# Routing weights of the first experts by broadcast transfers instead of a matrix product, with a third bank and longer rings

## Chip, cores and metric

The program runs on one core of a Trainium2 chip. The metric is the device time of one execution in microseconds (us), the median over the runs shown. The engines are named as in the profile: PE (matrix products; PEld is its weight load), DVE (vector), ACT (activation functions), POOL (the general engine), SP (which here only issues transfers).

## What is computed

A stack of eight blocks works on 2 x 1024 tokens of width 128, each block adding its normed result to the running stream. The change touches the sixth, a layer of experts:

```python
topk_w = topk_w / (topk_w.sum(-1, keepdims=True) + 1e-20)
combine_w = (jax.nn.one_hot(topk_idx, E, dtype=x.dtype) * topk_w[..., None]).sum(1)
g = jnp.einsum('th,eih->tei', x, gate_proj)
u = jnp.einsum('th,eih->tei', x, up_proj)
act = jax.nn.silu(g) * u
y = jnp.einsum('tei,ehi,te->th', act, down_proj, combine_w)
sg = x @ shared_gate_w.T
su = x @ shared_up_w.T
y = y + jax.nn.silu(sg) * su @ shared_down_w.T
```

There are E = 16 experts with 176 hidden rows each, and two shared experts (352 rows). Each token uses four of the sixteen, with the weights `combine_w`; the other twelve have weight zero. The kernel computes all sixteen for all tokens and multiplies by the weight, which is zero for most.

## The kernel before, in words

**Tiling.** The 16 x 176 + 352 hidden rows, padded, are 25 tiles of 128 rows (`R2`). The tokens are four chunks of 512 (`NC`, `CH`); chunks 0 and 1 are batch 0, chunks 2 and 3 are batch 1. The stage is one loop of 100 steps, i = 25 c + r: chunk c, tile r in the order `ORDER5`. The first three tiles of each chunk (`SHARED5 = 3`) are shared experts and need no routing weight; the other 22 are "weighted" steps. A tile of 128 rows holds rows of one expert or of two, since 176 is no multiple of 128: of the 22 tiles, 14 hold rows of two.

**A step.** fp32 values are split in a rounded part and a rest, so each product is three matmuls of 128 x 128 by 128 x 512. In step i, PE does the gate product (`pe_parts`, lines 1719 to 1721) into bank i % 2, the up product (the same lines) into bank 2 + i % 2, in a weighted step the spread (line 1768: a 0/1 matrix `SEL2` times the turned weights `CWT`, which copies each expert's weight of each token to all its rows, into bank 4), and then the down product of step i - 2 (`pe_hidden_parts`, lines 1725, 1726, 1728), which adds up over a chunk in bank 5. ACT takes the SiLU of the gate (line 1827, semaphore `sg`) and rounds the hidden value (line 1815, `hi`). DVE multiplies the SiLU by the weight (line 1874, `t`, reads bank 4), subtracts the rounded part of the step before (line 1863, the rest, `h`), and multiplies by the up product (line 1881, `p`), in that order. The times below speak of p(i), the start of line 1881 in step i. `um` says that the up product, and in a weighted step the spread, is done; `gm` says it of the gate; `dm` of the down product.

**What waits for what.** The rounded hidden value and its rest are rings of two (`HD5`, `HL5`), the SiLU a ring of two (`SG5`), the hidden value a ring of two (`PR5`). PE's gate of step i waits for `sg` of step i - 2, its up for `p` of step i - 2, the spread for `t` of the weighted step before, the down product of step i - 2 for `hi` and, ahead of its last matmul, for `h`. After the last tile of a chunk ACT copies bank 5 out (line 1819, `ot`, at r = 2 of the next chunk), and the down product of tile 0 of the next chunk waits for it.

**Other work in the loop.** `pe_beside_moe5`, `act_beside_moe5` and `dve_beside_moe5` insert, at fixed steps, the routing of batch 1 (DVE, chunk 0, r = 4, 8, 12, 16), the turning of the weights (PE and ACT, r = 1 for batch 0, r = 20 and 21 for batch 1), the norm of the finished chunk (DVE r = 5 and 6, then POOL, then PE's `pe_turn_x` at r = 9), and the attention features of the next block (PE r = 11 and 15, ACT r = 12 and 16, DVE r = 13 and 16; ACT changes its function table there and back). In chunk 2 PE also does `pe_lin_kv`, `pe_lin_out` and `pe_lin_proj` (r = 18, 20, 23).

**The weights.** `dve_route5_d` ends with the weights of a batch, in three bf16 parts (`dve_bf16_parts`, lines 1547 to 1550). PE turns them (line 1584), and ACT copies them to `CWT` (line 1590, `cwTs`).

**Transfers.** SP issues, in program order, the loads of this stage's matrices long before it, then during chunk 3 the loads of the eighth block's matrices (`moe3a`, `moe3b`, `r3w`), each behind a wait on PE's progress (`sp_late`). POOL splits them (lines 1686 and 1688) as they land.

Of the kernel before, what the change touches and what calls it, by code (L numbers as in the profile page):

```python
# [65 lines left out]
def sandwich(nc, x, w, cols, rows, rope, fc1q, fc2q, s2row, l1int, l2fc, r2w, r2b, moe2, moe2sel,  # L66
             r3w, r3b, moe3a, moe3b, consts, out):
    ctx = ExitStack()
    with ctx:
# [1079 lines left out]
        def sp_late(sp):  # L1149

            sp.wait_ge(A[1, "pv"], QH * KT * NG)
            for part, loads in enumerate((
                    ((LI, l1int),),
                    ((L2A, l2fc[:, 0:512]), (L2B, l2fc[:, 512:1024]), (arena(3328, 48), r2w), (arena(3376, H + D), r2b)),
                    ((MG, moe2[0]), (MU, moe2[1]), (MD, moe2[2]), (SEL2, moe2sel.bitcast(BF16))))):
# [1444 lines left out]
```

## Time and profile before

| | |
|---|---|
| median of 3 runs | 1651.7 us (1648.27 to 1655.72) |
| profiled execution, device time | 1657.76 us |
| its span in the trace | 1656.0 us |
| granted PE clock, mean of the span | 0.88 |
| the stage of the change, in the trace | 1111.3 to 1395.8 us |
| busy over the whole span: PE, DVE, ACT, POOL | 79%, 65%, 69%, 16% |

A busy share is the sum of the durations of an engine's instructions. PE's matmuls overlap, so that the distance between two starts says what one costs, not its duration. In a row of the timeline the bracket at the end gives the idle time before the instruction and what ended it.

### The profile page before, as it was taken

What the parts mean: (1) busy time and instruction counts of PE and PEld (TensorE: products, weight loads), DVE (VectorE), ACT (ScalarE), POOL (GpSimd) and SP (SyncE); (2) the same over time, 40 slices, a digit from 0 to 9 for tenths busy, and PEclk for the clock granted to TensorE, in tenths of its full rate; (3) what the DMA queues carried; (4) which work ended last, traced back from release to release, by engine and by line L of the source; (5) the groups of instructions that cost most, each with busy time, mean ns of one, the idle gap of its engine ahead of it and who ended that gap; (6) DMA issues with size and microseconds to landing.
All of it is one profiled execution on the core that took longest, in us unless ns stands there. A gap on an engine that the chain in (4) does not pass through costs nothing.

```text
span 1656.0 us, 22190 instructions
## 1 busy us (share of the span) xinstructions
PE 1315.9 (79%) x8121; PEld 659.1 (40%) x8156; DVE 1083.6 (65%) x2048; ACT 1147.4 (69%) x1619; POOL 261.9 (16%) x361
## 2 busy tenths in 40 slices
PE   5599988885777777777777696779998888787996
PEld 3233333353111111111111244466666666565774
DVE  6977777154446645664665645469876777676887
ACT  3166767655999999999999644444565455867884
POOL 4400003031000000000000123461101024611000
PEclk9589999997687887788788898879999989999998
DMA  5511110004210100010000210000000002000000
GB/s 191 136 22 21 29 34 4 1 1 111 80 20 0 20 19 1 20 20 0 20 1 0 111 58 0 1 1 1 1 1 1 1 13 96 1 1 1 7 8 13
DMA packets 22748, 44.07 MB, mean 27 GB/s; under 512 B 3248, under 2 KB 7600, under 8 KB 21872
## 3 DMA queue, kind: packets, MB, share of 16 engines
q1 hardware_dynamic: 21776, 41.09, 8.9%
q10 hardware_dynamic: 864, 1.57, 0.3%
q8 instruction: 64, 1.05, 0.3%
q14 instruction: 44, 0.36, 0.1%
HBM read 28.89 MB, written 13.76 MB: 26 GB/s over the span
## 4 chain that ended last, share of the span: by engine, by line
PE 43%; ACT 24%; DVE 19%; issue 11%; POOL 3%; ACTq 0%; DMA 0%; POOLq 0%; another core or an unknown queue 0%; DVEq 0%
ACT SHARED L1033 14%; PE PS L821 4%; PE PS L990 4%; PE PS L977 3%; DVE SHARED L1043 3%; DVE NM L730 3%; PE PS L1719 3%; PE PS L1721 3%; PE PS L1720 3%; PE PS L710 2%; PE PS L643 2%; PE PS L1725 2%; PE PS L785 2%; PE PS L1728 2%; PE PS L1726 2%
## 5 line engine op out<-in xcount | busy, mean ns | idle before, releaser
L1033 ACT ACTIVATE SHARED<-PS 128x1536 f32<-128x1536 f32 (+1 forms) x352 | 466.1, 1434 | 31.2 <-PE PS L977 30.2
L977 PE MATMUL PS<-QS,KS 51*128 51x512 bf16 (+1 forms) x1024 | 242.1, 461 | 134.1 <-ACT SHARED L1033 128.7
L1043 DVE TENSOR_TENSOR SHARED<-SHARED 128x1536 f32<-128x1536 f32 (+1 forms) x176 | 286.6, 1703 | 86.4 <-ACT SHARED L1033 86.4
L801 ACT ACTIVATE SHARED<-PS 128x512 f32<-128x512 f32 (+3 forms) x384 | 164.5, 493 | 99.3 <-PE PS L789 89.0
L977 PEld LDWEIGHTS PS<-QS,KS 51*128 51x128 bf16 (+1 forms) x1024 | 41.1, 99 | 386.8 <-ACT SHARED L1033 358.7
L990 PE MATMUL PS<-SHARED,Vg 128*16 128x512 f32 x1024 | 157.9, 694 | 1.7 <-DVE SHARED L1043 1.6
L730 DVE TENSOR_REDUCE NM<-PS 128x2 f32<-128x1024 f32 (+3 forms) x128 | 129.0, 1022 | 27.7 <-PE PS L716 19.6
L1719 PE MATMUL PS<-ROUNDED 128*128 128x512 f32 x328 | 141.6, 432 | 6.7 <-DVE SHARED L2194 3.5
L1721 PE MATMUL PS<-ROUNDED 128*128 128x512 f32 x328 | 132.3, 403 | 0.0
L1720 PE MATMUL PS<-ROUNDED 128*128 128x512 f32 x328 | 131.6, 401 | 0.0
L1827 ACT ACTIVATE KS<-PS 128x512 f32<-128x512 f32 x100 | 59.9, 599 | 84.8 <-PE PS L1721 84.3
L1725 PE MATMUL PS<-ROUNDED 128*128 128x512 f32 x228 | 109.0, 478 | 9.9 <-ACT SHARED L1819 6.1
L474 POOL COPY Vg<-XH 128x256 f32<-128x256 f32 x16 | 6.4, 402 | 628.6 <-PE PS L990 396.9
L324 POOL TENSOR_SCALAR VEY<-MVY 128x4 f32<-128x4 f32 x32 | 7.6, 237 | 619.8 <-DVE MVY L265 618.6
L821 PE MATMUL PS<-SHARED,Vg 128*16 128x256 f32 (+3 forms) x1152 | 96.0, 407 | 11.1 <-ACT SHARED L801 9.6
L2205 DVE TENSOR_TENSOR ROUNDED<-KS,ROUNDED 128x512 fp32r<-128x512 f32 x103 | 74.9, 731 | 42.4 <-ACT ROUNDED L2136 41.3
L2130 ACT ACTIVATE KS<-PS,C 128x512 f32<-128x512 f32 x103 | 71.1, 691 | 37.6 <-PE PS L1721 37.1
L1728 PE MATMUL PS<-ROUNDED 128*128 128x512 f32 x228 | 92.7, 407 | 4.3 <-DVE ROUNDED L2205 3.8
L710 PE MATMUL PS<-SHARED 48*128 48x512 bf16 (+3 forms) x384 | 72.0, 374 | 29.2 <-DVE NM L730 18.3
L1815 ACT ACTIVATE ROUNDED<-KS 128x512 fp32r<-128x512 f32 x100 | 62.9, 629 | 44.9 <-DVE KS L1881 44.2
L1874 DVE TENSOR_TENSOR SHARED<-KS,PS 128x512 f32<-128x512 f32 x88 | 60.1, 683 | 49.1 <-ACT KS L1827 45.8
L1726 PE MATMUL PS<-ROUNDED 128*128 128x512 f32 x228 | 91.3, 401 | 0.0
(280 smaller groups left out, 2352.2 us busy)
## 6 DMA issues: line engine op xcount, KB each, us to landing
qx<-SHARED SPq DMA_DIRECT2D x24, 256.0 KB, 4.0
SHARED<-in_moe SPq DMA_DIRECT2D x3, 1600.0 KB, 12.8
kx<-SHARED SPq DMA_DIRECT2D x18, 256.0 KB, 3.9
SHARED<-qx SPq DMA_DIRECT2D x16, 192.0 KB, 4.6
SHARED<-kx SPq DMA_DIRECT2D x16, 192.0 KB, 5.2
QS<-qx SPq DMA_DIRECT2D x16, 192.0 KB, 4.5
KS<-kx SPq DMA_DIRECT2D x16, 192.0 KB, 4.9
kx<-SHARED ACTq DMA_DIRECT2D x6, 256.0 KB, 5.2
```

The lines of the kernel that those rows point to most:

```text
L730: dve.tensor_reduce(out=dst, in_=src, axis=AX.X, op=ALU.max, negate=True).then_inc(A[0, "a_red"], 1)
L801: act.activation(PB[t % 3][:, h, q0:CH], bank(RING0[n % 3], q0), ACT.Exp, scale=SCORE_SCALE)\
L821: ins = pe.matmul(PS[32 * h:32 * h + VC, 6 * CH + a:6 * CH + b], Vg[g % 2][:, kt, h, :], PB[t % 3][:, h, a:b], start=kt == 0, stop=last an ...
L977: ins = pe.matmul(bank((v % 2) * GRP + f - a), KS[g % 2][r, h // 2, kt * P:kt * P + P], QS[g % 2][r, h // 2, qh * CH:(qh + 1) * CH], start ...
L990: ins = pe.matmul(PS[32 * h:32 * h + VC, 6 * CH:7 * CH], Vg[g % 2][:, kt, h, :], EX[:, f * CH:f * CH + CH], start=kt == 0, stop=kt == KT - 1)
L1033: act.activation(dst, PS[:, (v % 2) * GRP * CH:((v % 2) * GRP + b - a) * CH], ACT.Exp if second == qh else ACT.Sigmoid, scale=SCORE_SCALE)\
L1043: dve.tensor_tensor(ex_tile(j), ex_tile(j), GR[w % RING][:, 0:(b - a) * CH], ALU.mult)\
L1719: pe.matmul(dst, w[0], x[0], start=start, stop=False)
L1720: pe.matmul(dst, w[0], x[1], start=False, stop=False)
L1721: return pe.matmul(dst, w[1], x[0], start=False, stop=stop)
L1725: pe.matmul(dst, w[0], x[0], start=start, stop=False)
L1728: return pe.matmul(dst, w[0], x[1], start=False, stop=stop)
```

## The change

The spread on PE and its 0/1 matrix go away, and with them the three bf16 parts: the weights stay fp32 (`CW5`), are turned as fp32 by PE, copied by ACT into `WT5` (16 x 1024), and written by SP to DRAM (`wx`, 16 x 2048), once for each batch. For each of the 88 weighted steps SP then loads a 128 x 512 tile in which the row of an expert is repeated over the partitions of its rows: one transfer for each owner of the tile, so 36 a chunk and 144 in all. Four slots (`WB5`) form a ring: slot n is loaded when `p` of weighted step n - 4 is done. DVE multiplies the SiLU by the slot in place. Bank 4, now free, becomes a third bank of up products; `HD5`, `HL5` become rings of three, and the down products run three steps behind (`LAG5`). SP's loads of the eighth block stand between the weight loads of chunk 3, and `r3w` comes last.

```diff
+        wx = nc.dram_tensor("wx", (E2, TOK), F32, kind="Internal").ap()
-        SEL2 = ARENA[:, 13184:14784].bitcast(BF16)
+        WB5 = [arena(13184 + CH * i, CH) for i in range(3)] + [arena(32256, CH)]
...
+            def sp_experts7(r):
+                for name, part, dst, src in early.get(r, ()):
+                    sp.wait_ge(A[5, name], last + r)
+                    sp.dma_start(dst, src).then_inc(late_in[part], 16)
+            sp_weights_out5(sp, 0)
+            for c in range(NC):
+                for r in range(SHARED5, R2):
+                    sp_weights5(sp, c, r)
+                    if (c, r) == (1, SHARED5):
+                        sp_weights_out5(sp, 1)
+                    if c == NC - 1 and r >= SHARED5 + 4:
+                        sp_experts7(r - 4)
+            for r in range(R2 - 4, R2 + 1):
+                sp_experts7(r)
+            sp.wait_ge(A[5, "um"], N5)
+            sp.dma_start(SEL3, r3w.bitcast(BF16)).then_inc(late_in[4], 16)
...
-                ins = pe.transpose(bank(6).bitcast(BF16)[0:ROWS5, k * P:k * P + P],
-                                   CWB5[:, b * KT + k].rearrange("p c e -> p (c e)"), identb[:, :])
+                ins = pe.transpose(PS[0:E2, 6 * CH + k * P:6 * CH + k * P + P], CW5[:, b * KT + k], ident[:, :])
...
+        def sp_weights_out5(sp, b):
+            sp.wait_ge(A[5, "cwTs"], b + 1)
+            sp.dma_start(wx[:, b * S:b * S + S], WT5).then_inc(A[5, "wx"], 16)
+            sp.wait_ge(A[5, "wx"], 16 * (b + 1))
+
+        def sp_weights5(sp, c, r):
+            n = weighted(R2 * c + r)
+            slot = n % len(WB5)
+            if n >= len(WB5):
+                k, j = divmod(n - len(WB5), R2 - SHARED5)
+                sp.wait_ge(A[5, "p"], R2 * k + SHARED5 + j + 1)
+            for e, part in owners(r):
+                sp.dma_start(WB5[slot][part], wx[e:e + 1, c * CH:c * CH + CH].broadcast_to([part.stop - part.start, CH]))\
+                  .then_inc(w5_in[slot], 16)
...
-            own.link(dve.tensor_tensor(SEL5, SEL5, BEST5[:, :, 1:2].broadcast_to([P, KT, E2]), ALU.mult))
-            dve_bf16_parts(dve, own, SEL5, CWB5[:, b * KT:b * KT + KT], U5, E2).then_inc(A[5, "cw"], 1)
+            dve.tensor_tensor(CW5[:, b * KT:b * KT + KT], SEL5, BEST5[:, :, 1:2].broadcast_to([P, KT, E2]), ALU.mult)\
+               .then_inc(A[5, "cw"], 1)
...
+        LAG5 = 3
+        HL5 = [work_rounded(512 * i, 512) for i in range(LAG5)]
+        HD5 = [work_rounded(1536 + 512 * i, 512) for i in range(LAG5)]
...
-                if i >= 2:
-                    pe.wait_ge(A[5, "p"], i - 1)
-                ins = pe_parts(pe, bank(2 + i % 2), (MUH[:, k], MUL[:, k]), x, True, True)
-                if r >= SHARED5:
-                    if weighted(i):
-                        pe.wait_ge(A[5, "t"], weighted(i))
-                    if r == SHARED5:
-                        pe.wait_ge(A[5, "cwTs"], c // QH + 1)
-                    ins = pe.matmul(bank(4), SEL2[:, k], chunk(CWT, c), start=True, stop=True)
-                ins.then_inc(A[5, "um"], 1)
-                if i >= 2:
-                    down(i - 2)
+                if i >= 3:
+                    pe.wait_ge(A[5, "p"], i - 2)
+                pe_parts(pe, bank(2 + i % 3), (MUH[:, k], MUL[:, k]), x, True, True).then_inc(A[5, "um"], 1)
+                if i >= LAG5:
+                    down(i - LAG5)
...
                 dve.wait_ge(A[5, "sg"], i + 1)
-                dve.wait_ge(A[5, "um"], i + 1)
                 gate = SG5[i % 2]
                 if r >= SHARED5:
-                    if i >= 2:
-                        dve.wait_ge(A[5, "p"], i - 1)
-                    gate = TM5[i % 2]
-                    dve.tensor_tensor(gate, SG5[i % 2], bank(4), ALU.mult).then_inc(A[5, "t"], 1)
+                    slot, landed = weights_landed5(c, r)
+                    gate = WB5[slot]
+                    dve.wait_ge(w5_in[slot], landed)
+                    dve.tensor_tensor(gate, SG5[i % 2], gate, ALU.mult).then_inc(A[5, "t"], 1)
                 if i:
                     rest(i - 1)
...
+                dve.wait_ge(A[5, "um"], i + 1)
+                dve.tensor_tensor(PR5[i % 2], gate, bank(2 + i % 3), ALU.mult).then_inc(A[5, "p"], 1)
```

How it stands on PE at the border of chunks 0 and 1, before: the end of step r = 2 (down product of tile 0 of the new chunk, behind `S5_ot`), the whole of r = 3 with its spread, and the first matmul of the next down product.

```order
L1725 MATMUL PS<-ROUNDED 128x512 [waits S5_ot,S5_hi]
L1726 MATMUL PS<-ROUNDED 128x512
L1728 MATMUL PS<-ROUNDED 128x512 [waits S5_h]
L1719 MATMUL PS<-ROUNDED 128x512 [waits S5_sg]
L1720 MATMUL PS<-ROUNDED 128x512
L1721 MATMUL PS<-ROUNDED 128x512
L1719 MATMUL PS<-ROUNDED 128x512 [waits S5_p]
L1720 MATMUL PS<-ROUNDED 128x512
L1721 MATMUL PS<-ROUNDED 128x512
L1768 MATMUL PS<-SHARED 128x512 [waits S5_cwTs,S5_t]
L1725 MATMUL PS<-ROUNDED 128x512 [waits S5_hi]
```

The same place in the changed kernel (lines 1757 to 1759 are `pe_parts`, 1763 to 1766 `pe_hidden_parts`):

```order
L1763 MATMUL PS<-ROUNDED 128x512 [waits S5_hi]
L1764 MATMUL PS<-ROUNDED 128x512
L1766 MATMUL PS<-ROUNDED 128x512 [waits S5_h]
L1757 MATMUL PS<-ROUNDED 128x512 [waits S5_sg]
L1758 MATMUL PS<-ROUNDED 128x512
L1759 MATMUL PS<-ROUNDED 128x512
L1757 MATMUL PS<-ROUNDED 128x512 [waits S5_p]
L1758 MATMUL PS<-ROUNDED 128x512
L1759 MATMUL PS<-ROUNDED 128x512
L1763 MATMUL PS<-ROUNDED 128x512 [waits S5_ot,S5_hi]
L1764 MATMUL PS<-ROUNDED 128x512
```

The wait for `ot` now stands behind the gate and up products of r = 3, and the spread with its two waits is gone.

On DVE, the first two weighted steps of the stage, before:

```order
L1874 TENSOR_TENSOR SHARED<-KS,PS 128x512 [waits S5_p,S5_um,S5_sg]
L1863 TENSOR_TENSOR ROUNDED<-KS,ROUNDED 128x512 [waits S5_hi]
L1881 TENSOR_TENSOR KS<-SHARED,PS 128x512 [waits S5_h,S5_t]
L1874 TENSOR_TENSOR SHARED<-KS,PS 128x512 [waits S5_p,S5_um,S5_sg]
L1863 TENSOR_TENSOR ROUNDED<-KS,ROUNDED 128x512 [waits S5_hi]
```

And in the changed kernel (1904 is the product with the weight, 1894 the rest, 1912 the product with up):

```order
L1904 TENSOR_TENSOR SHARED<-KS,SHARED 128x512 [waits w5_in0,S5_sg]
L1894 TENSOR_TENSOR ROUNDED<-KS,ROUNDED 128x512 [waits S5_hi]
L1912 TENSOR_TENSOR KS<-SHARED,PS 128x512 [waits S5_um,S5_h,S5_t]
L1904 TENSOR_TENSOR SHARED<-KS,SHARED 128x512 [waits w5_in1,S5_sg]
L1894 TENSOR_TENSOR ROUNDED<-KS,ROUNDED 128x512 [waits S5_hi]
```

Three operations as before, in the same order; the first waits for a transfer where it waited for `um`, and both its operands now lie in SBUF.

On SP, the last issues of chunk 3 in the changed kernel (before, the loads of the eighth block stood alone, with `r3w` ahead of the third `moe3b`):

```order
L1173 DMA SHARED<-in_moe3b 128x1024 [waits S5_um]
L1624 DMA SHARED<-wx 80x512 [waits S5_p]
L1624 DMA SHARED<-wx 48x512
L1173 DMA SHARED<-in_moe3a 128x1024 [waits S5_gm]
L1624 DMA SHARED<-wx 128x512 [waits S5_p]
L1173 DMA SHARED<-in_moe3b 128x1024 [waits S5_um]
L1173 DMA SHARED<-in_moe3a 128x2048 [waits S5_gm]
L1173 DMA SHARED<-in_moe3b 128x2048 [waits S5_um]
L1185 DMA SHARED<-in_r3w 128x1024 [waits S5_um]
```

## Rows read from the trace of the kernel before

**Rows 1.** Busy time of the engines over the stage (last line of the windows view)

```profile
sum 284.50, PE 259.79 PEld 188.69 DVE 220.54 ACT 150.52 POOL 46.15; mean PE 64.95 PEld 47.17 DVE 55.13 ACT 37.63 POOL 11.54
```

**Rows 2.** Tile view: two of DVE's operations; durations min/median/max in ns

```profile
L1863 DVE TENSOR_TENSOR ROUNDED<-KS,ROUNDED x100: 657/685/1654, 1116.8 to 1394.5; 128x512 fp32r<-128x512 f32 x100
L1874 DVE TENSOR_TENSOR SHARED<-KS,PS x88: 654/686/690, 1121.3 to 1391.7; 128x512 f32<-128x512 f32 x88
```

**Rows 3.** Timeline of PE, a plain step of chunk 1: start, duration

```profile
1229.89 0.39 PE L1768 MATMUL PS<-SHARED 128*128 128x512 bf16 x1
...
1232.22 0.39 PE L1768 MATMUL PS<-SHARED 128*128 128x512 bf16 x1
```

**Rows 4.** Timeline of DVE, p of two neighbouring steps of chunk 0

```profile
1129.01 0.68 DVE L1881 TENSOR_TENSOR KS<-SHARED,PS 128x512 f32<-128x512 f32 x1
...
1131.00 0.68 DVE L1881 TENSOR_TENSOR KS<-SHARED,PS 128x512 f32<-128x512 f32 x1
```

**Rows 5.** Windows between p's (line 1881): length, busy time, p's within, PE clock

```profile
1125.55:1165.31 39.76, 10.88 (x16) 1.00 0.00 1
1165.31:1175.18 9.87, 2.72 (x4) 1.00 0.00 0
1181.44:1185.19 3.75, 0.68 (x1) 1.00 0.00 0
1185.19:1227.97 42.78, 9.53 (x14) 1.00 0.00 1
1227.97:1243.07 15.10, 4.76 (x7) 1.00 0.00 1
1295.86:1316.65 20.79, 4.76 (x7) 1.00 0.00 1
1327.30:1331.67 4.37, 0.68 (x1) 0.56 0.00 2
1331.67:1378.55 46.88, 10.20 (x15) 0.93 0.08 24
1378.55:1393.08 14.53, 4.06 (x6) 1.00 0.14 43
```

**Rows 6.** Timeline of PE behind the copies of bank 5, chunks 1 and 3

```profile
1181.38 0.47 PE L1725 MATMUL PS<-ROUNDED 128*128 128x512 f32 x1 [1.31 <-ACT SHARED L1819]
...
1325.79 0.76 PE L1725 MATMUL PS<-ROUNDED 128*128 128x512 f32 x1 [3.48 <-ACT SHARED L1819]
```

**Rows 7.** Timeline of PE, turn of x in chunk 1

```profile
1200.72 0.66 PE L395 MATMUL PS<-ident,XN 128*128 128x128 f32 x4 [0.36 <-POOL XN L336]
```

**Rows 8.** Timeline of ACT, features of chunk 1, first and last row

```profile
1209.78 1.28 ACT L1461 ACT_TABLE_LOAD   x1
...
1214.47 0.60 ACT L1827 ACTIVATE KS<-PS 128x512 f32<-128x512 f32 x1
```

**Rows 9.** Timeline of the first weights: DVE's parts, ACT's copy, first weighted step

```profile
1112.58 0.23 DVE L1547 CAST SHARED<-SHARED 128x128 bf16<-128x128 f32 x1
...
1113.42 0.29 DVE L1550 TENSOR_TENSOR SHARED<-SHARED 128x128 bf16<-128x128 f32 x1
...
1117.14 1.02 ACT L1590 ACTIVATE SHARED<-PS 51x1024 bf16<-51x1024 bf16 x1 [0.46 <-PE PS L1584]
...
1120.15 2.99 POOL L1714 TENSOR_TENSOR ROUNDED<-XH,ROUNDED 128x512 fp32r<-128x512 f32 x2
1121.26 0.67 DVE L1874 TENSOR_TENSOR SHARED<-KS,PS 128x512 f32<-128x512 f32 x1
...
1122.03 1.65 DVE L1863 TENSOR_TENSOR ROUNDED<-KS,ROUNDED 128x512 fp32r<-128x512 f32 x1
```

**Rows 10.** Transfers: tensor, queue, count, KB each, median us from issue to landing

```profile
SHARED<-in_s2row SPq DMA_DIRECT2D x1, 256.0 KB, 9.8
...
SHARED<-in_r3w SPq DMA_DIRECT2D x1, 256.0 KB, 2.8
...
mx<-MT SPq DMA_DIRECT2D x8, 16.0 KB, 2.2
```

More of the change, by code:

```diff
@@ L63, with sandwich @@
 NW = 18
-def sandwich(nc, x, w, cols, rows, rope, fc1q, fc2q, s2row, l1int, l2fc, r2w, r2b, moe2, moe2sel,
+def sandwich(nc, x, w, cols, rows, rope, fc1q, fc2q, s2row, l1int, l2fc, r2w, r2b, moe2,
              r3w, r3b, moe3a, moe3b, consts, out):
@@ L1138, in work_rounded @@
             return rounded(WORK + at, n)
+        w5_in = [sem(f"w5_in{i}") for i in range(len(WB5))]
         f0_in = sem("f0_in")
-        N_LATE = (1, 4, 4, 2, 3, 2)
+        N_LATE = (1, 4, 3, 2, 3, 2)
         late_in = [sem(f"late_in{i}") for i in range(len(N_LATE))]
@@ L1571, in pe_logits @@
             ins.then_inc(A[5, "lg"], 1)
-        ROWS5 = 3 * (E2 + 1)
         def act_scores5(act, b):
@@ L1589, in act_turn_weights5, with owners, weights_landed5 @@
             act.wait_ge(A[5, "cwT"], b + 1)
-            act.activation(CWT[0:ROWS5, b * S:b * S + S], bank(6).bitcast(BF16)[0:ROWS5, :], ACT.Copy)\
-               .then_inc(A[5, "cwTs"], 1)
+            if b:
+                act.wait_ge(A[5, "wx"], 16 * b)
+            act.activation(WT5, PS[0:E2, 6 * CH:8 * CH], ACT.Copy).then_inc(A[5, "cwTs"], 1)
+        def owners(r):
+            k = ORDER5[r]
+            cuts = [(e, max(k * P, e * I2), min(k * P + P, e * I2 + I2)) for e in range(E2)]
+            return [(e, slice(a - k * P, z - k * P)) for e, a, z in cuts if a < z]
+        def sp_weights_out5(sp, b):
[11 more added lines that the diff above has]
+                  .then_inc(w5_in[slot], 16)
+        def weights_landed5(c, r):
+            n = weighted(R2 * c + r)
+            done = [(k, j) for k in range(NC) for j in range(SHARED5, R2)][0:n + 1]
+            return n % len(WB5), 16 * sum(len(owners(j)) for m, (k, j) in enumerate(done) if m % len(WB5) == n % len(WB5))
         def dve_clear5(dve, own):
             own.mark(dve.memset(CWT_ALL, 0.0))
-            own.mark(dve.memset(CWB5[:, :, 0, 16:17], 1.0))
-            own.mark(dve.memset(CWB5[:, :, 1:3, 16:17], 0.0))
             own.mark(dve.memset(SCAN5, 1.0))
@@ L1880, in dve_moe5 @@
                     dve.wait_ge(A[5, "h"], i - 1)
-                dve.tensor_tensor(PR5[i % 2], gate, bank(2 + i % 2), ALU.mult).then_inc(A[5, "p"], 1)
+                dve.wait_ge(A[5, "um"], i + 1)
+                dve.tensor_tensor(PR5[i % 2], gate, bank(2 + i % 3), ALU.mult).then_inc(A[5, "p"], 1)
                 dve_beside_moe5(dve, own, c, r)
```

47 lines of the change are left out of this document (19 added, 28 removed).

## The prediction

> **What bounds the kernel now.** I read the windows view of the stage first. Over its 284.5 us DVE is busy for 220.5 and PE for 259.8 [rows 1], but PE's durations overlap, so the distance between starts has to be read. In a plain weighted step the spread starts at 1229.89 and again at 1232.22 [rows 3]: ten matmuls in 2.33 us, 0.23 each, and PE sets the pace. In the busy part of chunk 0 the starts of p are 1.99 apart [rows 4], with DVE's three operations end to end: DVE sets the pace. A step costs 2.33 where PE leads the way and 1.99 where DVE does, so the reader has to know which of the two each stretch belongs to. The windows cut at the starts of p tell it [rows 5]:
>
> - chunk 0, r = 5 to 20, 16 steps, 39.76: 16 x 1.99 = 31.8, and the rest is the routing of batch 1 on DVE. DVE-bound.
> - chunk 0, r = 21 to 24, 4 steps, 9.87: PE-bound (2.3 each and the turned weights).
> - r = 3 of chunk 1: 3.75, of chunk 3: 4.37. PE stands still for 1.31 and 3.48 behind ACT's copy of bank 5 [rows 6]; in chunk 3 its clock then falls from 2.4 to 1.2 GHz (mean 0.56 in that row). Chunk 2's r = 3 is like chunk 1's.
> - chunk 1, r = 4 to 17, 14 steps, 42.78: mixed. DVE works on the norm, PE waits for POOL's XN [rows 7], and ACT changes tables and computes features from 1209.78 to 1214.47, in which no SiLU is made [rows 8]. Chunk 2 has the same length.
> - chunk 1, r = 18 to 24: 15.10; chunk 2, r = 18 to 24: 20.79, longer by PE's own extra work.
> - chunk 3, r = 4 to 18, 15 steps, 46.88; r = 19 to 24: 14.53.
>
> **The change part by part.** PE loses one matmul of ten in 88 steps: 88 x 0.23 = 20.2 us of PE time. DVE loses nothing in a step: three operations before and after. So a plain step can fall from 2.33 to 9 x 0.233 = 2.10 and no lower than DVE's 1.99. Only where PE leads does the removed matmul count. The third up bank and the rings of three let PE finish about one step more before it must stop, which counts where DVE or ACT stalls.
>
> (a) *The first weights.* Before, ACT's copy ends at 1118.16 [rows 9], the spread can follow, and the first product with the weight starts at 1121.26. Now a write to DRAM, its wait, and a load lie between. I allow 0.3 for turning fp32 instead of bf16, 2.2 for the write (as mx<-MT), 0.2 for SP's two wake-ups, and 3.3 for the load, which is the 2.8 of r3w, the nearest row (same 128 rows of 2 KB, from the same queue) [rows 10], and 0.5 for the loads issued right behind it, which share its engines. 1118.2 + 6.0 = 1124.2, so 2.9 late. DVE is held in order: the rest of step 2, p(3) and all behind them wait, and the DVE-bound stretch follows, so nothing hides it. But the rest of step 2 took 1.65 for 0.69 beside POOL's work, which ends at 1123.1; later it is past that: 1.0 back. Net +1.9. By r3w's 2.8 alone it is +1.4, by the 9.8 of s2row +8.4.
>
> (b) *The three bf16 parts* go from the chain of weights: 1112.58 to 1113.71 [rows 9]. For batch 0 this is ahead of a PE-bound moment and gives nothing; for batch 1 it is in the DVE-bound stretch: -1.1.
>
> (c) *End of chunk 0*: PE has a lead there from the DVE-bound stretch and keeps it at 2.10 against 1.99, so four steps at DVE's pace, 8.0 for 9.87: -1.9.
>
> (d) *Borders.* `ot` is waited for one step later, behind gate and up of r = 3, so ACT's copy is covered. 3.75 falls to about 2.1 in chunks 1 and 2, 4.37 to 2.0 in chunk 3: -1.6, -1.6, -2.4. In chunk 3 PE still waits some 2.8 us (DVE is slow there), but DVE no longer waits for PE.
>
> (e) *r = 4 to 17 of chunks 1 and 2.* Fourteen times 0.23 would be 3.2. I take less, since two chains pin the stretch. PE's turn at r = 9 needs XN from POOL, which needs DVE's norm at r = 5 and 6: PE waited 0.36 for it [rows 7], and a faster PE waits longer. Then ACT's 4.7 us of features [rows 8] start as soon as they did relative to r = 12. What is left is r = 4 to 6 (0.9, less for the lead is short) and r = 11, 12, 15, 16, some 0.6: -1.5 each, -3.0.
>
> (f) *r = 18 to 24 of chunk 1*: 15.10 to 7 x 1.99 = 13.9, since ACT's stall at r = 16 leaves PE a step ahead: -1.2.
>
> (g) *The same of chunk 2*: 20.79 is 7 x 2.33 and 4.5 of extra products. Now 7 x 2.10 + 4.5 = 19.2, less the lead of a step and a quarter, 2.6: 16.6, so -4.2. Without the lead it is -1.6.
>
> (h) *Chunk 3, r = 4 to 18*: six PE-bound steps at its start, less one wait, -1.1; r = 17 and 18 behind a DVE-bound stretch, -1.5; the middle waits on DVE and ACT: 0. Sum -2.6.
>
> (i) *r = 19 to 24*: 14.53, POOL splits the next weights. PE would give 6 x 0.23 = 1.4. Against it, the rest (two operands in SBUF) rises from 0.69 to 1.65 beside POOL, the product with the weight (one in PSUM) never passes 0.69 [rows 2], and the changed one has both operands in SBUF. I take 0; four steps slowed by 0.4 and no gain would be +1.6. The Trainium skill says why in "SBUF — State Buffer", section "SBUF: two separate sides": a VectorE operation with two SBUF inputs and a GpSimd one exclude each other, whoever starts first. The rows bear it out for the rest, and by the rule the changed product is exposed too; by the rule (i) would be +1.6, by the row of the old product -1.4.
>
> The steady transfers cost nothing if they land in time. Slot n is free at the end of p(n - 4) and needed at the start of the product three steps later: 3 x 2.1 = 6.2 us. SP wakes and issues one or two transfers, 0.8; with 2.8 for landing that is 3.6, so 2.6 to spare. In chunk 3 a 512 KB load stands between two. Most of a landing is fixed, since 16 KB take 2.2 and 256 KB 2.8 [rows 10], so 512 KB cost some 1.3 more, still inside; if they cost r3w's 2.8 twice, one step waits 3.0. `r3w` now lands last of the late loads; it was needed by nobody before POOL's splits resume, some 10 us after the last up product. ACT's and PE's semaphore counts are unchanged, and the drain after step 99 is the same chain.
>
> **Sum**: 1.9 - 1.1 - 1.9 - 5.6 - 3.0 - 1.2 - 4.2 - 2.6 = -17.7 us. The profiled execution took 1657.8, which gives 1640.1; it lies 6.1 above the median of 1651.7, and the same gain from the median gives **1634.0**.
>
> **Rivals.** *Transfers land late* (slower). Nothing in the trace reads one row 128 times. If a landing takes L, a ring of four gives a period of (L + 0.8 + 2.0) / 4 a step. It starts to bind at L = 5.6 and eats the gain at a mean step of (284.5 - 25 - 6) / 88 = 2.88 (the stage of [rows 1] less the twelve shared steps and some 6 for its first step and its drain), L = 8.7. With s2row's 9.8, queued behind eight loads, it is 3.15: 88 x 0.27 = 24 us slower, 1676. For it speaks only that row; against it r3w's 2.8. 0.10.
>
> *The latency chains hold everything* (no change). Removing the matmul makes DVE, POOL's XN and ACT's tables the bound everywhere: (e) and (h) give 0, (g) 1.6, (a) costs 4, and (i) 1.6. Then -1.1 - 1.9 - 5.6 - 1.2 - 1.6 + 5.6 = -5.8: 1646. For it: 39.76 us of chunk 0 are DVE-bound already. 0.14. A slower read of one row comes to the same place: 2.5 us for 256 KB would lie under the mean step of the new stage, (284.5 - 17.7 - 6) / 100 = 2.6, but above the 2.0 to 2.1 of the plain ones, and take back about 0.45 in 20 such steps, 9 us: 1643. The Trainium skill, "DMA: Bandwidth & Descriptors", section "Latency and other measured facts", has copies whose rows collide in HBM at 103 GB/s, which is an estimated 2.5 us for a slot, and says the cause is inferred; no run here shows it. 0.06, by r3w.
>
> *PE-bound throughout* (faster than forecast): leads last, all 20.2 of PE's time and 7 us of waits come back: -27, 1625. Against it DVE's share in chunk 0. 0.08.
>
> **The numbers.** Forecast 0.62, with its own range 1627 to 1642. The whole range leaves out the slow transfers and the edge of the others: 1624 to 1649. A measurement of this kernel tells about 0.5% (8 us) from no change. Faster than 1643.4: 0.62 + 0.08 + half of the slow reads and a little of the chains, 0.76; within: 0.14; slower: 0.10.
>
> **What would show it.** In the profile after: p's 2.1 or less apart in plain weighted steps; the first product with a weight near 1124 where the stage starts at 1111; no wait behind line 1819's successor at r = 3; DVE waiting for a transfer once, not 88 times; the product with the weight longer than 0.69 beside POOL in the last steps. The prediction is wrong if wx loads take over 5.6 us, if PE's clock falls in the first wait and stays down, or if the stage after it, whose first steps POOL feeds, starts later against the end of this one.

## The result, and the profile after

The changed kernel takes 1645.72 us (median of 20 runs, 1638.19 to 1655.25) where the kernel before takes 1656.17 (20 runs, the first three among them). The ratio is 0.9948, 95% interval 0.9928 to 0.9967; it compares the means, 1646.86 and 1655.48, and leaves out one slow run of the kernel before (1886.79). That is 8.6 us faster, 5.5 to 11.9 (the medians lie some 10 apart). The forecast was 17.7 us: right in sign, about twice too large. The time lies inside the whole range (1624 to 1649) and outside the forecast's own (1627 to 1642). The kernel before also came out 4.5 us above the 1651.7 of its first three runs, which makes up part of the distance between 1634.0 and 1645.7.

The profiled executions have spans of 1656.0 and 1643.9 us. From here on "the stage" is the time from the start of the first product p to the start of the last (line 1881 before, 1912 after): 278.77 us before, 266.02 after, 12.75 less. It is the measure for all runs below, because the first p starts anywhere from 1108.1 to 1119.2 us in the thirteen profiles of this study, in no order that follows the edits, so what lies ahead of the stage says nothing about them.

The windows view after, cut at the starts of p as in [rows 5] (length, DVE's busy time for line 1912, PE clock, DMA share, GB/s):

```profile
1129.34:1167.95 38.61, 10.88 (x17) 0.96 0.40 111
1167.95:1175.91 7.96, 2.73 (x5) 1.00 0.39 124
1182.09:1184.07 1.98, 0.68 (x1) 1.00 0.00 0
1184.07:1229.48 45.41, 9.51 (x14) 0.92 0.30 82
1229.48:1243.41 13.93, 4.76 (x8) 1.00 0.42 118
1251.57:1295.75 44.18, 9.52 (x14) 0.96 0.29 84
1295.75:1311.67 15.92, 4.77 (x8) 1.00 0.44 116
1322.31:1324.30 1.99, 0.68 (x2) 0.50 0.04 8
1324.30:1368.45 44.15, 10.19 (x16) 0.95 0.33 95
1368.45:1382.20 13.75, 4.08 (x6) 1.00 0.76 230
```

Every row is shorter than its partner in [rows 5], save two: r = 4 to 17 of chunk 1 (45.41 for 42.78) and of chunk 2 (44.18 for 42.78). In both the clock of PE is no longer 1.00. (It is 0.96 in r = 5 to 20 of chunk 0 too, but there DVE sets the pace: three later runs with a clock of 1.00 in this stretch take the same 38.6.) By the terms of the prediction, in us:

| term | forecast | measured |
|---|---|---|
| (a) first weights | +1.9 | +1.92 |
| (b) bf16 parts, r = 5 to 20 | -1.1 | -1.15 |
| (c) end of chunk 0 | -1.9 | -1.91 |
| (d) three borders | -5.6 | -5.91 |
| (e) r = 4 to 17, chunks 1, 2 | -3.0 | **+4.03** |
| (f) r = 18 to 24, chunk 1 | -1.2 | -1.17 |
| (g) the same, chunk 2 | -4.2 | -4.87 |
| (h) chunk 3, r = 4 to 18 | -2.6 | -2.73 |
| (i) r = 19 to 24 | 0 | -0.78 |
| r = 0 to 2 of chunks 1 to 3 | 0 | -0.18 |
| sum | -17.7 | -12.75 |

(e) is 7.0 us off, all others together 2.1 us better than forecast. So the question is what happens in r = 4 to 17. Cut further, the loss lies in three steps: r = 4 to 8 take 13.50 (before 14.17), r = 9 to 11 take 10.59 and 9.37 in the two chunks (before 7.19 and 7.19), r = 12 to 17 take 21.3 (before 21.4). The timeline of PE around the turn of x in chunk 1 shows where (start, duration, in brackets the wait and who ended it):

```profile
1195.70 0.49 PE L1766 MATMUL PS<-ROUNDED 128*128 128x512 f32 x1 [0.24 <-DVE ROUNDED L1894]
1200.10 1.12 PE L396 MATMUL PS<-ident,XN 128*128 128x128 f32 x4 [3.90 <-POOL XN L337]
1200.87 0.78 PE L1757 MATMUL PS<-ROUNDED 128*128 128x512 f32 x1
1201.44 0.63 PE L1758 MATMUL PS<-ROUNDED 128*128 128x512 f32 x1
1201.87 0.63 PE L1759 MATMUL PS<-ROUNDED 128*128 128x512 f32 x1
...
1205.28 0.63 PE L1758 MATMUL PS<-ROUNDED 128*128 128x512 f32 x1
1205.71 0.57 PE L1759 MATMUL PS<-ROUNDED 128*128 128x512 f32 x1
1206.12 0.40 PE L1757 MATMUL PS<-ROUNDED 128*128 128x512 f32 x1
```

PE stands still for 3.90 us at the turn, where it stood for 0.36 [rows 7]. Behind that its matmuls take 0.63 at starts 0.43 apart, and 0.40 at 0.23 apart only from 1206.12 on. The granted clock says the same: it is 0.50 (1.2 GHz) from 1199.26, 3.1 us into the wait, to 1206.08, 6.0 us beyond its end. In chunk 2, with a wait of 3.89, it is 0.50 from 1267.52 to 1270.94, 3.3 us beyond the end. ACT and DVE are held by it, since the gate of r = 10 stands behind the turn:

```profile
1202.53 0.60 ACT L1858 ACTIVATE KS<-PS 128x512 f32<-128x512 f32 x1 [3.62 <-PE PS L1759]
...
1203.16 0.69 DVE L1904 TENSOR_TENSOR SHARED<-KS,SHARED 128x512 f32<-128x512 f32 x1 [2.84 <-ACT KS L1858]
...
1206.95 0.69 DVE L1904 TENSOR_TENSOR SHARED<-KS,SHARED 128x512 f32<-128x512 f32 x1 [1.90 <-ACT KS L1858]
```

The wait has two parts. Measured from p of r = 8 (1199.41 before, 1197.57 after), PE was at the turn 0.95 us after it before (1200.36) and is there 1.37 ahead of it now (1196.20): 2.3 us earlier. And XN, which ended 1.26 after p of r = 8, ends 2.47 after it: 1.2 later. That second part is POOL's. Its timeline after, and then before:

```profile
1190.03 0.54 POOL L325 TENSOR_SCALAR VEY<-MVY 128x4 f32<-128x4 f32 x1 [66.28 <-DVE MVY L266]
1190.66 1.33 POOL L326 TENSOR_TENSOR RSY<-VEY,ROOT 128x4 f32<-128x4 f32 x1
1194.56 0.57 POOL L332 TENSOR_SCALAR NMX<-MVX 128x4 f32<-128x4 f32 x1 [2.57 <-DVE MVX L266]
...
1196.94 3.10 POOL L337 TENSOR_SCALAR XN<-X,NMX,RSX 128x128 f32<-128x128 f32 x4
```

```profile
1192.28 0.19 POOL L324 TENSOR_SCALAR VEY<-MVY 128x4 f32<-128x4 f32 x1 [69.13 <-DVE MVY L265]
1192.55 1.01 POOL L325 TENSOR_TENSOR RSY<-VEY,ROOT 128x4 f32<-128x4 f32 x1
1196.40 0.23 POOL L331 TENSOR_SCALAR NMX<-MVX 128x4 f32<-128x4 f32 x1 [2.84 <-DVE MVX L265]
...
1198.50 2.17 POOL L336 TENSOR_SCALAR XN<-X,NMX,RSX 128x128 f32<-128x128 f32 x4
```

The same four XN instructions take 3.10 us for 2.17, a 128 x 4 one 0.54 for 0.19. Nothing of POOL's work was edited; what runs beside it was: DVE's product with the weight now reads both operands from SBUF, and transfers land there. Which of the two slows POOL, the run with SiLU in PSUM tells. In this execution the product itself is hardly longer (tile view, min/median/max in ns; compare [rows 2]):

```profile
L1904 DVE TENSOR_TENSOR SHARED<-KS,SHARED x88: 656/685/775, 1126.1 to 1379.9; 128x512 f32<-128x512 f32 x88
```

The first weights, timeline after:

```profile
1119.01 1.02 ACT L1604 ACTIVATE Vg<-PS 16x1024 f32<-16x1024 f32 x1 [0.49 <-PE PS L1597]
...
1120.12 0.34 SPq L1614 DMA_DIRECT2D wx<-Vg  x1
...
1122.04 2.68 SPq L1624 DMA_DIRECT2D SHARED<-wx  x6
...
1126.13 0.69 DVE L1904 TENSOR_TENSOR SHARED<-KS,SHARED 128x512 f32<-128x512 f32 x1 [2.94 <-DMA SHARED<-wx]
```

From the end of ACT's copy to the product it is 6.1 us (forecast 6.0): 1.9 for write and wait, 4.1 for the load. It is the only wait of DVE for a transfer in the whole stage. The transfers' own table (KB each, median us to landing) gives

```profile
SHARED<-wx SPq DMA_DIRECT2D x32, 256.0 KB, 3.3
...
SHARED<-wx SPq DMA_DIRECT2D x16, 224.0 KB, 3.1
```

### The profile page after: what moved, and what is told of

Same layout as the page of the kernel before. It is cut to its first block, busy times and chain, and to the rows that moved or that the text cites. A ratio compares the mean times of both kernels' runs of the same rounds, so it can differ in the third digit from the quotient of the medians.

```text
span 1643.9 us, 22175 instructions
## 1 busy us (share of the span) xinstructions
PE 1301.3 (79%) x8053; PEld 664.0 (40%) x8068; DVE 1081.1 (66%) x2038; ACT 1141.9 (69%) x1619; POOL 270.8 (16%) x361
## 3 DMA queue, kind: packets, MB, share of 16 engines
HBM read 51.14 MB, written 13.89 MB: 40 GB/s over the span
## 4 chain that ended last, share of the span: by engine, by line
PE 39%; ACT 25%; DVE 18%; issue 12%; POOL 4%; DMA 2%; SPq 0%; ACTq 0%; POOLq 0%; DVEq 0%
ACT SHARED L1034 15%; PE PS L822 4%; PE PS L991 4%; PE PS L978 3%; DVE NM L731 3%; DVE SHARED L1044 2%; PE PS L1757 2%; PE PS L644 2%; PE PS L711 2%; PE PS L1759 2%; PE PS L1758 2%; PE PS L786 2%; PE PS L1208 2%; DVE KS L1912 2%; PE PS L1766 2%
## 5 line engine op out<-in xcount | busy, mean ns | idle before, releaser
L1757 PE MATMUL PS<-ROUNDED 128*128 128x512 f32 x328 | 143.2, 437 | 9.8 <-ACT KS L1858 4.4
L1759 PE MATMUL PS<-ROUNDED 128*128 128x512 f32 x328 | 133.3, 406 | 0.0
L1758 PE MATMUL PS<-ROUNDED 128*128 128x512 f32 x328 | 132.7, 404 | 0.0
L1766 PE MATMUL PS<-ROUNDED 128*128 128x512 f32 x228 | 93.4, 409 | 14.6 <-DVE ROUNDED L1894 12.0
L1763 PE MATMUL PS<-ROUNDED 128*128 128x512 f32 x228 | 92.8, 407 | 4.8 <-ACT SHARED L1850 3.3
L1764 PE MATMUL PS<-ROUNDED 128*128 128x512 f32 x228 | 91.7, 402 | 0.0
L786 PE MATMUL PS<-SHARED 50*128 50x512 bf16 (+3 forms) x384 | 80.9, 336 | 4.8 <-ACT SHARED L802 4.3
```

The source lines that it names most:

```text
L786: ins = pe.matmul(bank(at, q0), K0[g % 3][r, p, kt * P:kt * P + P], Q0[g % 3][r, p, qh * CH + q0:qh * CH + CH], start=True, stop=not diag)
L1757: pe.matmul(dst, w[0], x[0], start=start, stop=False)
L1758: pe.matmul(dst, w[0], x[1], start=False, stop=False)
L1759: return pe.matmul(dst, w[1], x[0], start=False, stop=stop)
L1766: return pe.matmul(dst, w[0], x[1], start=False, stop=stop)
```

## The experiments

Two theories stood against each other for (e). **The stall**: PE comes to the turn too early, XN too late, and the clock falls behind the wait. **The new steps**: the three-step lag or the transfers cost something in these steps by themselves. The first experiments take away or test one thing each.

**The turn of x two steps later.**

```diff
-            if c and r == (17 if c == 3 else 9):
+            if c and r == (17 if c == 3 else 11):
                 pe_turn_x(pe, edges[6], c - 1)
-            if c in (1, 2) and r == 11:
+            if c in (1, 2) and r == 13:
                 pe_lin_features(pe, c - 1, 0)
```

and in the same way the rest that follows it on PE, ACT and DVE (chunks 1 and 2 by two steps, the second features and chunk 2's products by one).

> The changed kernel with PE's turn of x in chunks 1 and 2 moved from step r = 9 to 11, and what follows it moved with it (ACT's copy 10 to 12; features PE 11 and 15 to 13 and 16, ACT 12 and 16 to 14 and 17, DVE 13 and 16 to 15 and 17; in chunk 2 kv 18 to 19, out 20 to 21, ACT's copy of it 21 to 22). Theory A (the faster PE reaches the turn some 4 us before POOL has XN, stands still for 3.9 us and is then clocked at 1.2 GHz): the wait at line 396 in chunks 1 and 2 falls from 3.9 to under 0.5, the clock stays at 2.4 GHz, and r = 4 to 17 of the two chunks fall from 45.4 and 44.2 to 41 to 42 each; time 0.990 of the kernel before (the changed kernel: 0.9948). Rival (DVE and ACT hold that stretch and the wait is only where it shows): both stay at 44 to 45 and the time at 0.995.

Measured: 1635.58 us (6 runs), ratio 0.9873 (0.9838 to 0.9908). Stage 259.08, 6.9 less than the change's. In the windows view of this run r = 9 to 11, r = 4 to 17 and r = 18 to 24 of chunk 1 are

```profile
1191.51:1197.56 6.05, 2.04 (x4) 1.00 0.47 127
1178.01:1214.77 36.76, 9.52 (x14) 1.00 0.34 95
1214.77:1231.46 16.69, 4.76 (x7) 1.00 0.41 111
```

No wait at the turn, clock 1.00. In chunk 1 8.65 us are gained in r = 4 to 17 and 2.76 given back behind it, where ACT's features now fall: 5.9 net. In chunk 2 it is 7.41 and 2.77: 4.6 net. Part of what r = 4 to 17 gained beyond the 41 to 42 expected is this shift. Chunk 3 gives 3.5 back. 1.9 of it is in r = 19 to 24 (15.69 for 13.75), where DVE's product and rest are longer beside POOL (up to 1.16 and 1.78 us). The other 1.5 is in r = 6 and 7, behind another turn of x, at which PE waits 2.39 us for its XN. The windows view gives r = 6 and 7 of chunk 3 (p of r = 5 to p of r = 7) for this run and for three that follow below: with twelve added matmuls, with distinct rows, with two up banks.

```profile
1311.75:1318.91 7.16, 1.36 (x2) 0.76 0.44 108
1321.67:1328.83 7.16, 1.36 (x3) 0.76 0.36 109
1323.57:1329.16 5.59, 1.36 (x3) 1.00 0.39 100
1327.94:1333.52 5.58, 1.36 (x2) 1.00 0.42 102
```

PE's wait for that XN is 2.39, 2.40, 2.37 and 1.42 us. In the first two runs the clock falls behind it, in the other two it does not. So after the same wait the fall of the clock costs 1.6 us.

**The kernel before with the same later turn**, the control for it (the same diff on the kernel before).

> The kernel before, with only the turn of x and what follows it two steps later, as in the run of the change with the later turn (which took 6.9 us off the stage). Theory A (the later turn there repairs a stall that the change made: PE waited 0.36 us for XN before and 3.9 after): the kernel before gains at most 2 us of its stage of 278.8, ratio 0.998 to 1.001. Rival (the turn stands too early in either kernel, and the gain has nothing to do with the change): the kernel before gains 5 to 7 us too, ratio 0.996 or less.

Measured: ratio 1.0005 (0.9984 to 1.0026), stage 277.76, 1.0 less than before's. By itself the later turn is worth 1.0 us in the stage and nothing that the timed runs show; it repairs what the change broke.

**Work for PE while it waits.** In chunks 1 and 2, twelve matmuls into bank 7, which is free there, ahead of the turn; their result is read by nobody.

```diff
+            if c in (1, 2) and r == 9:
+                for _ in range(12):
+                    pe.matmul(bank(7), MGH[:, 0:P], chunk(hR, c), start=True, stop=True)
             if c and r == (17 if c == 3 else 9):
                 pe_turn_x(pe, edges[6], c - 1)
```

> The changed kernel with 12 dummy matmuls (128x512 into bank 7, results unused) ahead of PE's turn of x in chunks 1 and 2, which fill 2.8 of the 3.9 us of idle time. It tells the clock's part from the wait's: if the slow clock after the wait costs by itself, r = 10 and 11 of chunk 1 fall from 4.73 and 3.79 to about 3.6 and 2.1, and r = 10 of chunk 2 likewise, r = 4 to 17 from 45.4 to about 43 and from 44.2 to 43. If the wait alone costs, both stay within 0.3.

Measured: 1643.25 us in its one execution, stage 263.85. The turn, and the matmuls behind it:

```profile
1193.83 2.69 PE L1820 MATMUL PS<-ROUNDED 128*128 128x512 f32 x11
1197.65 0.66 PE L396 MATMUL PS<-ident,XN 128*128 128x128 f32 x4 [1.13 <-POOL XN L337]
1198.06 0.47 PE L1757 MATMUL PS<-ROUNDED 128*128 128x512 f32 x1
1198.38 0.39 PE L1758 MATMUL PS<-ROUNDED 128*128 128x512 f32 x1
```

XN comes at the same time after p of r = 8 (2.48; 2.47 without), so nothing is gained in waiting, but the clock stays at 2.4 GHz. r = 9 to 11 fall from 10.59 and 9.37 to 7.81 and 7.81: **the fall of the clock costs 2.8 and 1.6 us**, where the granted clock stood at 0.50 for 6.0 and 3.3 us behind the wait. It is not the whole loss: before it was 7.19. The stage gains only 2.2 us, since chunk 3 gives 2.0 back: 1.5 behind the wait shown above, 0.5 in r = 19 to 24.

**The product with one operand in PSUM.** ACT writes the SiLU over the gate in its PSUM bank, DVE reads it there, and PE waits for that product before it writes the bank again.

```diff
-                act.activation(SG5[i % 2], bank(i % 2), ACT.Silu).then_inc(A[5, "sg"], 1)
+                act.activation(bank(i % 2) if r >= SHARED5 else SG5[i % 2], bank(i % 2), ACT.Silu).then_inc(A[5, "sg"], 1)
...
-                    dve.tensor_tensor(gate, SG5[i % 2], gate, ALU.mult)
+                    dve.tensor_tensor(gate, bank(i % 2), gate, ALU.mult)
...
                     pe.wait_ge(A[5, "sg"], i - 1)
+                    if (i - 2) % R2 >= SHARED5:
+                        pe.wait_ge(A[5, "t"], weighted(i - 1))
```

> The changed kernel with ACT writing the SiLU of the weighted steps back into the gate's bank in PSUM, so that the product with the weight reads one operand from PSUM and one from SBUF; PE's gate then also waits for that product of two steps before. Theory B (the new product with two SBUF operands and POOL exclude each other, so POOL's XN comes later): the time from the end of DVE's statistics to the end of XN in chunk 1 falls from 5.6 back to about 4.4 us, PE's wait at the turn from 3.9 to about 2.7, and the last steps of chunk 3 beside POOL (r = 23, 24, 2.9 each) to about 2.4. If POOL is slow for another reason nothing of this changes. The stretch DVE-bound stays at 1.99 a step.

Measured: 1637.56 us in one execution, stage 257.30, 8.7 less than the change's. POOL in chunk 1:

```profile
1188.88 0.20 POOL L325 TENSOR_SCALAR VEY<-MVY 128x4 f32<-128x4 f32 x1 [66.46 <-DVE MVY L266]
1189.16 1.01 POOL L326 TENSOR_TENSOR RSY<-VEY,ROOT 128x4 f32<-128x4 f32 x1
...
1195.10 2.17 POOL L337 TENSOR_SCALAR XN<-X,NMX,RSX 128x128 f32<-128x128 f32 x4
```

These are the durations of the kernel before, to 0.01 us, with the same transfers landing beside them, so it was the product's second operand and not the transfers that slowed POOL. XN ends 1.26 after p of r = 8 again, PE waits 1.37, the clock stays at 1.00, and r = 9 to 11 take 6.59 and 6.57. Against the 7.81 of the run before, with the same clock: **POOL's slower work costs 1.2 us a chunk**, and without it and the clock's fall the three steps are 0.6 below the kernel before. The wait is 2.5 us shorter than the change's and not only 1.2, because PE also comes later (0.05 ahead of p of r = 8 for 1.37): its gate now waits for the product of two steps before. That the clock stays up is due to both. In chunk 3, where DVE and POOL work side by side too, r = 4 to 18 fall from 44.15 to 42.09. The last steps did not get shorter as expected (13.89 for 13.75), and r = 18 to 24 of chunk 2 take 0.7 more (16.65).

It was timed later, in five runs:

> The run with SiLU in PSUM again, now timed: its stage was 257.3 us in one look. By the stage alone it should be 21.5 us under the kernel before and 8.7 under the change: ratio 0.985 to 0.989. If the product with an operand in PSUM only shifts waits, the profiled stage is back over 262 and the ratio near 0.994.

1633.24 us, ratio 0.9862 (0.9835 to 0.9890), stage 258.14: 22.9 us under the kernel before by the timed runs (18 to 27), 20.6 by the stage.

**What each part of the change is worth.** Down products three steps behind alone, on the kernel before:

```diff
-                if i >= 2:
-                    down(i - 2)
+                if i >= LAG5:
+                    down(i - LAG5)
```

with rings of three for HL5 and HD5.

> The kernel before with the down products three steps behind and rings of three for the rounded value and its rest alone (two up banks, the spread on PE and its bf16 weights as they were). By my terms this gives the borders: r = 3 of chunks 1 and 2 from 3.75 to about 2.3, of chunk 3 from 4.37 to about 2.3, 5 us in all, and nothing in the plain steps (2.31 stays). p of step 0 to p of step 99: from 278.8 to about 274. If the lead of PE needed the third bank or the spread's removal too, it gives under 2 us.

Measured: 1648.31 us (10 runs), ratio 0.9954 (0.9927 to 0.9980), stage 273.65, so -5.1. The borders give -1.60, -1.58 and -2.39, term (d) nearly whole; chunk 3's r = 4 to 18 give -1.8, and r = 12 to 17 of chunks 1 and 2 take 1.1 back each. There the granted clock is 0.92: in chunk 1 PE stands for 1.96 us before 1218.51, the clock is 0.50 from 1218.97 to 1222.38, and r = 15 and 16 take 2.36 and 3.41 for 1.98 and 2.65. The kernel before has the same wait (1.94) and keeps its clock.

The transfers alone (the change with `LAG5 = 2` and `bank(2 + i % 2)`):

> The change without its down products three steps behind and without its third up bank: the weights come by transfers, the spread is gone from PE, but the rings hold two and there are two up banks. Stage here means the time from the first to the last product p: 278.8 us before, 266.0 with the whole change. Theory A (the lost term (e) comes from the routing weights themselves: a PE without the spread reaches the turn of x early, stands, falls to 1.2 GHz, and POOL's XN takes 3.1 us in place of 2.2 beside a product whose two operands lie in SBUF): r = 4 to 17 of chunks 1 and 2 stay at 44 to 46 us each, the borders r = 3 stay at about 3.5, 3.5 and 4.2, stage about 272, ratio 0.996 to 0.999. Theory B (the loss in (e) comes from down products three steps behind): r = 4 to 17 falls under 42 in both chunks, stage about 267, ratio near 0.993.

Measured: ratio 0.9989 (0.9969 to 1.0009), which is not to be told from no change; stage 274.92, -3.9, where 272 was expected. r = 4 to 17 take 43.90 and 44.31, both over the 42.78 of before, r = 9 to 11 take 7.81 (7.19 before) and r = 12 to 17 take 22.05 and 22.41 (21.42): with neither lag nor third bank, term (e) has the wrong sign already. (In r = 12 to 17 the clock is 0.92 here too.) Its XN takes 3.10 in chunk 2, and PE waits

```profile
1263.46 0.66 PE L396 MATMUL PS<-ident,XN 128*128 128x128 f32 x4 [1.81 <-POOL XN L337]
```

behind which the clock stays up. So the slower POOL comes with the transfers and the product that reads them; the fall of the clock at the turn comes with the lag, as the next run shows.

The change with two up banks (`bank(2 + i % 2)`):

> The whole change without its third up bank (two banks, rings of three, down products three steps behind, weights by transfers). If the third bank carries little: stage 266 to 267.5, within 1.5 us of the whole change, PE waiting at most some tenths for p in front of its up products. If it is what gives PE its lead in (c) and (g): r = 21 to 24 of chunk 0 back over 8.5 and r = 18 to 24 of chunk 2 over 17.5, stage about 270.

Measured: ratio 0.9972 (0.9945 to 0.9998), stage 268.66, between the two expectations. PE waits in two places, in chunk 1 1.95 us for p and 2.13 for XN, the clock falls, and r = 9 to 11 take 9.39 and 9.33: lag and transfers are enough for that, without the third bank. The third bank is worth 2.6 us: 1.1 in (c) (9.09 for 7.96), 1.2 in (g) (17.16 for 15.92), 1.0 in (i), less 0.7 in (e). In steps of the stage, each from one profiled execution, then: transfers -3.9, lag -6.3, third bank -2.6.

**The repeated row.** The loads read 128 different rows, of another tensor, where they read one row of `wx` 128 times. The routing weights are left out by it.

```diff
-                sp.dma_start(WB5[slot][part], wx[e:e + 1, c * CH:c * CH + CH].broadcast_to([part.stop - part.start, CH]))\
+                sp.dma_start(WB5[slot][part], moe2[0][part, c * CH:c * CH + CH])\
```

> The whole change, but the 88 loads read 128 different rows of 2 KB (of the gate's weights) where they read one row of wx 128 times; the write to wx and its wait stay. Left out: the routing weights don't reach the product. If reading one row over and over is what makes a 256 KB load land in 3.3 us (r3w's distinct rows: 2.8), the 256 KB loads land in about 2.8 here; if the 3.3 comes from loads at a pace of one in 2 us, they stay at 3.1 to 3.5. Either way the stage keeps its 266.0 us within 0.5, but for its first step, which can start up to 0.5 earlier.

```profile
SHARED<-in_moe SPq DMA_DIRECT2D x32, 256.0 KB, 2.7
...
SHARED<-in_moe SPq DMA_DIRECT2D x16, 224.0 KB, 2.6
```

The same load lands in 2.7 us for 3.3. The run changes the tensor along with the rows, so that repeating a row costs the 0.6 is likely, not shown. Only the first load shows it: the steps to p of r = 3 take 10.15 for 11.17, more than the 0.5 expected. The rest of the stage keeps its length (265.45 in all).

**Both repairs together.** Later turn and SiLU in PSUM, and then the same with the turn and the first features only one step later and the second features where they were:

> The whole change, with the turn of x and what follows it two steps later and the SiLU written into the gate's PSUM bank, so that the weight's product has one operand in PSUM. Each alone made the stage 259.1 and 257.3 us where the whole change has 266.0. Theory A: both act on the same wait at the turn, so they overlap in chunks 1 and 2, and only the part in chunk 3 (r = 4 to 18: 42.1 for 44.2) adds to the later turn: stage 255 to 257.5, ratio 0.984 to 0.987. Rival: the two are independent and add up: stage 250.4, ratio 0.981 or less. Other rival: the gate's bank is held until the weight's product has read it, which costs PE more once it isn't waiting elsewhere: stage over 259.

> SiLU in the gate's PSUM bank, and the turn of x, its copy and the first features one step later, not two; the second features stay at r = 15 and 16. With XN ready some 14.6 us after p of r = 3 and PE at r = 10 at about 15.3, PE should not wait at the turn. If the +2 of the run before only pushed ACT's features into r = 18 to 24 (they took 16.7 and 19.4 there, for 13.9 and 15.9), this one should give back part: r = 4 to 17 about 38.5, r = 18 to 24 of chunk 1 about 15, stage 252 to 255, ratio 0.984 to 0.988. If the first and second features now stand too close (three steps), r = 12 to 17 rises over 20 and the stage is over 256.

Measured: stage 253.76 and 256.03, ratios 0.9879 (0.9847 to 0.9911) and 0.9882 (0.9854 to 0.9910). PE waits for XN at neither turn of chunks 1 and 2. The gains overlap for the most part, as expected (3.5 us beyond the better of the two alone; adding up would have given 250.4). By the stage the first is the best of all, 25.0 us under the kernel before; the timed runs can't tell it from SiLU in PSUM alone (0.9862), which is the smaller edit. With the turn one step later r = 4 to 17 take 39.58 and r = 18 to 24 of chunk 1 14.26, where two steps give 36.93 and 16.66: over both stretches 53.8 and 53.6. The sign set for features that stand too close came true (r = 12 to 17 over 20, at 20.34, and the stage over 256), though 1.4 of the 2.3 us between the two runs lie in r = 19 to 24 of chunk 3 (14.16 for 12.78).

## Why the prediction was right in sign and wrong in size

**Right, term by term.** (a) to (d), (f), (g), (h) came within 0.7 us each, and they carry the mechanism: the matmul's removal, the border, the lead. The first weights came 6.1 us after ACT's copy for 6.0; the rest of step 2 fell to 0.68 as its start moved past POOL's work. The end of chunk 0 ran at DVE's pace, 7.96 for 8.0. The borders fell to 1.98, 1.99 and 1.99, in chunk 3 with PE at 1.2 GHz (0.50 in its row), DVE no longer waiting for it. The transfers were free after the first: *transfers land late* fell (3.3 us, 5.6 needed to bind), and so did *slower read of one row*: steps of 1.99 went on beside loads of 3.3. (The 6.2 us of room were 3 x 2.1 = 6.3; nothing hangs on it.) The Trainium skill, "DMA: Bandwidth & Descriptors", section "Latency and other measured facts", has 103 GB/s for copies whose rows lie 4 or 8 MiB apart in HBM. Here 118 GB/s were moved over r = 18 to 24 of chunk 1 with no wait for a load, so the trace does not bear that figure out for one row read over and over.

**The step that failed is (e).** It said that PE "waited 0.36 for it" and that "a faster PE waits longer", that ACT's features then start as they did, and that "What is left is ... -1.5 each". Two things are wrong in it.

1. XN was taken as fixed against DVE's norm. It isn't: it came 1.2 us later against p of r = 8, since POOL's instructions took 3.10 for 2.17 beside a product with two SBUF operands. The run with SiLU in PSUM shows it (2.17 again). In (i) this sharing was weighed, but only as a cost to DVE; the 1.2 that it costs POOL wasn't in any term. What it costs DVE differs from one run to the next. In the change's own profile the product never passed 0.78 us in 88, and (i) came to -0.78. But in all five other runs with both operands in SBUF it took up to 1.16 to 1.19 us in the last steps of chunk 3, and r = 19 to 24 took 14.27 to 15.89 (14.53 before). So the 0 taken for (i) lies inside the spread, and -0.78 is luck. From the run with twelve added matmuls:

```profile
1371.08 1.62 POOL L1726 TENSOR_TENSOR ROUNDED<-SHARED,ROUNDED 128x512 fp32r<-128x512 f32 x1
1372.06 1.19 DVE L1907 TENSOR_TENSOR SHARED<-KS,SHARED 128x512 f32<-128x512 f32 x1
```

The product that starts 0.98 behind POOL is the one that is stretched. The Trainium skill, "SBUF — State Buffer", section "SBUF: two separate sides", says that of a VectorE operation with two SBUF inputs and a GpSimd one that reads SBUF the first to start takes the shared ports and the other is held. The trace agrees: POOL pays too where it starts second (its 1.80 at 1377.05, 0.05 behind a product, is 1.30 in the run with one operand in PSUM).
2. A longer wait was costed at nothing. But PE carries the gates that DVE and ACT need next, and after standing for 3.90 and 3.89 us it ran at 1.2 GHz for 6.0 and 3.3 us: 2.8 and 1.6 us, shown by the twelve matmuls that keep it busy. The prediction named such a fall ("if PE's clock falls in the first wait and stays down") for the stage's first wait, and read one in chunk 3 ([rows 5], [rows 6]: a wait of 3.48, then 0.56), but (e) has no term for it.

Together 2 x 1.2 + 2.8 + 1.6 = 6.8 of the 7.0. In the remaining steps r = 4 to 8 gave 0.67 a chunk, as forecast for r = 4 to 6, and r = 12 to 17 gave 0.1 for some 0.6: they are ACT's chain, table and features. Without the fall and POOL's delay r = 9 to 11 gave 0.6, so (e) would have been about -2.7, close to the -3.0; in the whole run with SiLU in PSUM it was -3.45 (41.16 and 40.95 for 42.78). So *the latency chains hold everything* was right in r = 12 to 17 only.

**Not settled.** The stage lost 12.75 us and the timed runs 8.6 (at most 11.9). In part this is the choice of executions: the two profiled ones are 12.0 us apart, since they lie 2.3 above the mean of the kernel before and 1.1 below the change's, and single runs of either scatter over 16 to 17 us. The run with two up banks has such a gap as well (10.1 by the stage, at most 9.1 timed), the other seven timed runs have none: the stage's gain lies inside their intervals (19.7, 20.6 and 25.0 us among them). The two with the gap are those whose clock falls at the turn. The run with distinct rows, which has the same wait (3.88), took 9.38 and 10.43 in r = 9 to 11 where the change took 10.59 and 9.37, with the clock at 0.50 for 3.4 us in chunk 1 and 6.8 in chunk 2 where the change has 6.8 and 3.4. So the time at 1.2 GHz differs from one execution to the next. That it is longer on average than in the profiled one would narrow the gap, but this was not measured.

## What to carry to other kernels

When an edit makes an engine faster, follow it to its next wait for a third engine, and cost the wait by what stands behind it in that engine's order and by the clock at which PE comes out of it, not by the wait alone; then try the waiting step later (here two steps, 6.9 us off the stage, and chunk 3 shows that the next wait has to be followed in the same way). And when an operand moves from PSUM to SBUF in a DVE operation, price it on POOL's instructions beside it, not only on DVE's. Here undoing that one operand (SiLU left in PSUM) took the gain from 8.6 us to 22.9 by the timed runs, from 12.8 to 20.6 by the stage.

## What the runs showed of the hardware

- DVE's fp32 product of 128 x 512 with both operands in SBUF takes the same 0.685 us at the median as with one in PSUM, but up to 1.19 where it starts about 1 us behind a POOL instruction (with one operand in PSUM at most 0.69). POOL's work beside it grows too: four 128 x 128 instructions from 2.17 to 3.10 us, one of 128 x 4 from 0.19 to 0.54, and back to 2.17 and 0.20 with one operand in PSUM. POOL's busy time in the whole kernel rose from 261.9 to 270.8 us with the same 361 instructions.
- DVE's fp32r subtraction, two SBUF operands as well, did stretch beside POOL: 1.60 and 1.59 us in r = 23 and 24 of chunk 3. There it started 0.74 us behind an instruction of POOL's each time (1377.79 and 1380.68 against 1377.05 and 1379.94), while the product (1377.00 and 1379.91, 0.69 and 0.68 us) had started 0.05 and 0.03 ahead of the same two. That the later of the two pays fits these four rows and the two of the run with twelve added matmuls; no run was made for it.
- A load of 256 KB that repeats one 2 KB row of DRAM 128 times lands in 3.3 us, one of 128 different rows of another tensor in 2.7, both issued about every 2 us.
- The same wait of 2.4 us is followed by a fall of the clock to 1.2 GHz in two runs and not in a third; r = 6 and 7 of chunk 3 then take 7.16 us for 5.59.
